# Attention block with two layer norms: two chunks of the rotation move to GpSimd, and the written-out order changes

## The chip, the core and the metric

The kernel runs on one core of a Trainium2 chip. The metric is device time in microseconds (us), from one launch to its end. The engines are TensorE (PE; its weight loads are PEld), VectorE (DVE), ScalarE (ACT), GpSimd (POOL) and SyncE (SP), which here only issues DMAs.

## What is computed

One transformer layer on 2048 tokens of width 128, all in float32: causal attention with 16 heads of width 8 and rotary positions, a residual and a layer norm, then a dense layer with int4-rounded weights plus a low-rank term, a residual and a layer norm.

```python
qkv = einsum('bsd,ed->bse', x, W_qkv)            # x: (1, 2048, 128)
q, k = rope(q), rope(k)                          # pairs of neighbours rotated
scores = q @ k.T / sqrt(8), causal               # 16 heads, 2048 x 2048
out = softmax(scores) @ v                        # the maximum of each row is subtracted
x = layernorm(x + out @ W_o.T)                   # no scale, eps 1e-5
w = clip(round(kernel / s), -8, 7) * s           # s = max|kernel| / 7
x = layernorm(x + x @ w + bias + (x @ a) @ b)
```

## The kernel before

**Tiling.** The tokens are cut into 4 chunks of 512 (`NC`, `CH`), each of 4 tiles of 128, the heads into 4 groups of 4 (`HG`). A task is the queries of one chunk for one group; the last one (group 3, chunk 0) is halved, which makes 17 tasks, 0 to 16. Groups 0 and 2 go through the chunks upwards, 1 and 3 downwards (`TASKS`).

**Two passes over the scores.** Pass A finds each query's maximum: TensorE writes the scores, queries on partitions, into one of two slots of two PSUM banks (`ring`), and VectorE reduces 1024 columns at once (`row_max`, L896). One such piece is a unit; there are 273. Units on the diagonal need the causal mask. In tasks 0 to 3 TensorE adds it by a bfloat16 matmul into the same bank (L1075, L1079); in tasks 4 to 16 (`VECTOR_MASKS`) VectorE adds it while it takes the maximum, one operation a part (`masked_max`, L870). When a task's units are done, its maxima are transposed, split into two parts and written by GpSimd's DMA into extra rows of the query operand (event M: `rows`, `load_maxima`, L749). Then pass S computes the scores again, keys on partitions, with the maximum subtracted by those rows: TensorE writes a set of one or two heads into one of three banks (`sT`, L1110), ScalarE takes the exponential (L814), GpSimd zeroes the masked half of diagonal pieces (L740), and PV multiplies by the values (L1125) into one bank. O normalises (L1134, L940, L942). For group 3 the steps POST 2 to 5 and NORM 0 and 1 follow, with the reciprocal root on GpSimd (`post_rstd`, L712, L715) and the bias there (`post_bias`, L720).

**The start.** TensorE transposes the weights and chunk 0, ScalarE copies them out, and per chunk c and operand w (q, k) come P (two projections, L1035, plain and with neighbours swapped), the two multiplications by cosine and sine (`rotate`, DVE L850), R (their sum, L664), H and T (high part on ScalarE, rest on GpSimd) and E (rows placed by a selecting matmul, L1050). D stores the parts to DRAM, G loads them for the later groups. X and V are a chunk's transpose and values.

**The order.** `schedule()` writes one list of events by a beam search: `Course` keeps times for each engine by constants (LOAD, COLUMN, `maxima_time`, LANDING), and of the candidates those with the least idle time, weighted by `WEIGHTS`, are kept. Every engine walks through that list and executes its part of each event in order, waiting on semaphores. Thus a wait of any instruction holds up all that is behind it on its engine. W, the scale of the int4 weights, is put behind the event PV 1 0, and on GpSimd stands between masks. A POST 3 or 5 also places `post_rstd` on GpSimd's queue at that same place of the list.

## Time and profile before

| | us |
|---|---|
| median of 3 runs (478.73 to 485.3) | 483.12 |
| the profiled execution | 482.48 |
| its span, first to last instruction | 480.7 |
| DVE busy in it | 396.8 |
| ACT busy in it | 311.4 |
| PE busy in it, by modelled ends | 444.2 |

What lies around the span is 1.8 us. The mean granted TensorE clock is 0.955 of full speed. Matmuls overlap, so PE's busy time is no measure of its load; what tells is which wait ends last. The page's DVE time counts overlapping instructions once.

### The profile page before, as it was taken

The numbers are of one execution on the slowest core, as the hardware profiler recorded it, in microseconds if no ns is written. First come the engines' busy times: TensorE is split into PE (matmuls) and PEld (weight loads), VectorE is DVE, ScalarE is ACT, GpSimd is POOL, SyncE is SP. The second block draws the span as 40 slices with busy tenths as digits, with TensorE's granted clock in tenths as the row PEclk, the third lists the DMA queues.
The fourth block names the chain that finished last, engine by engine and source line by source line (L and its number), as shares of the span: only waits on it lengthen the run. The fifth ranks groups of instructions, "written<-read, shape, count | busy, mean of one in ns | idle before, by whom it ended". The sixth has DMA issues, their size and how long they took to land.

```text
span 480.7 us, 8224 instructions
## 1 busy us (share of the span) xinstructions
PE 444.2 (92%) x2914; PEld 200.1 (42%) x2914; DVE 396.8 (83%) x827; ACT 311.4 (65%) x630; POOL 108.1 (22%) x178
## 2 busy tenths in 40 slices
PE   4988799699799999999999999999999999999972
PEld 2445454334343344343434543434344434434542
DVE  1789689789989999999889999998999989933466
ACT  2324467278067868778778786767786788689610
POOL 8543511201100030020303311030002002442343
PEclk9999879899969999999999999999999999999975
DMA  7322211110000001110000011100000000000001
GB/s 240 143 89 89 91 39 54 54 54 24 3 0 2 1 14 55 55 54 14 3 2 3 14 55 55 54 11 1 1 2 3 1 3 2 3 24 1 22 1 44
DMA packets 11576, 16.54 MB, mean 34 GB/s; under 512 B 1820, under 2 KB 6700, under 8 KB 11536
## 3 DMA queue, kind: packets, MB, share of 16 engines
q1 hardware_dynamic: 10448, 15.75, 9.2%
q0 software_dynamic: 1088, 0.28, 0.3%
q8 instruction: 23, 0.38, 0.3%
q14 instruction: 17, 0.14, 0.1%
HBM read 10.37 MB, written 5.24 MB: 32 GB/s over the span
## 4 chain that ended last, share of the span: by engine, by line
PE 72%; DVE 10%; issue 9%; ACT 4%; POOL 2%; DMA 2%; SPq 0%; POOLq 0%; DVEq 0%; ACTq 0%
PE sT L1110 26%; PE oP L1125 23%; PE ring L1068 13%; DVE pmax L896 8%; ACT probs L814 3%; PE sT L1035 2%; PE ring L1134 1%; DMA qS<-mrows 1%; PE oP L1035 1%; PE sT L1050 1%; PE ring L1154 1%; DMA a_sb<-in_L_ffn_a_dram 1%; DVE summed L870 1%; POOL rstd L715 1%; POOL probs L740 1%
## 5 line engine op out<-in xcount | busy, mean ns | idle before, releaser
L814 ACT ACTIVATE probs<-sT 128x512 f32<-128x512 f32 (+2 forms) x576 | 285.9, 581 | 92.8 <-PE sT L1110 91.6
L896 DVE TENSOR_REDUCE pmax<-ring 128x2 f32<-128x1024 f32 (+2 forms) x212 | 248.7, 1220 | 29.4 <-PE ring L1068 26.4
L1110 PE MATMUL sT<-qS,kS 64*128 64x512 f32 (+3 forms) x648 | 193.1, 423 | 6.4 <-ACT vP L772 2.8
L1068 PE MATMUL ring<-kS,qS 64*128 64x512 f32 (+3 forms) x640 | 152.9, 428 | 7.6 <-DVE pmax L896 5.7
L1110 PEld LDWEIGHTS sT<-qS,kS 64*128 64x128 f32 x648 | 97.2, 191 | 128.3 <-ACT probs L814 107.6
L1125 PE MATMUL oP<-probs,vP 128*9 128x512 f32 (+3 forms) x1296 | 146.7, 532 | 2.0 <-POOL probs L740 1.9
L1068 PEld LDWEIGHTS ring<-kS,qS 64*128 64x128 f32 x640 | 71.0, 190 | 51.3 <-DVE pmax L896 27.4
L870 DVE CUSTOM_DVE_ANT_0 summed<-ring,tail_mask 128x128 bf16<-128x128 f32 (+3 forms) x192 | 81.5, 486 | 8.1 <-PE ring L1068 7.5
L740 POOL TENSOR_SCALAR_AFFINE_SELECT probs<-probs 128x512 f32<-128x512 f32 x64 | 40.2, 634 | 199.1 <-ACT probs L814 198.9
L749 POOL DMA_DIRECT2D qS<-mrows x34 | 19.7, 582 | 98.5 <-DVE mrows L916 94.6
L1125 PEld LDWEIGHTS oP<-probs,vP 128*9 128x9 f32 x1296 | 20.4, 88 | 42.3 <-issue 23.2
L823 ACT COPY oT<-oP 128x512 f32<-128x512 f32 (+1 forms) x17 | 9.7, 568 | 19.7 <-PE oP L1125 19.7
L870 DVE DVE_READ_ACCUMULATOR2_ANT pmax<- 128x1 f32 x192 | 15.9, 83 | 0.0
L796 ACT CAST qp<-rot 128x512 fp32r<-128x512 f32 x4 | 2.5, 618 | 17.5 <-POOL rot L664 12.0
L940 DVE RECIPROCAL rsum<-ring 128x16 f32<-128x16 f32 (+1 forms) x17 | 4.1, 241 | 10.8 <-PE ring L1134 10.7
L1134 PE MATMUL ring<-ident,oT 128*128 128x128 f32 x64 | 10.6, 287 | 2.4 <-DVE pmax L896 1.3
L664 POOL TENSOR_TENSOR rot<-rot 128x512 f32<-128x512 f32 x6 | 7.6, 1267 | 20.1 <-DVE rot L850 18.1
L1134 PEld LDWEIGHTS ring<-ident,oT 128*128 128x128 f32 x64 | 7.0, 143 | 8.4 <-DVE pmax L896 5.7
L850 DVE TENSOR_TENSOR rot<-oP,cs 128x512 f32<-128x512 f32 x4 | 2.7, 685 | 9.3 <-PE oP L1035 9.2
L715 POOL TENSOR_TENSOR rstd<-rstd,mhalf 128x4 f32<-128x4 f32 (+1 forms) x10 | 9.2, 916 | 0.8
L850 DVE TENSOR_TENSOR rot<-sT,cs 128x512 f32<-128x512 f32 x12 | 8.0, 684 | 1.5 <-PE sT L1035 1.5
L712 POOL TENSOR_SCALAR rstd<-mv 128x4 f32<-128x4 f32 (+1 forms) x10 | 2.3, 231 | 26.6 <-DVE mv L973 26.6
(126 smaller groups left out, 209.1 us busy)
## 6 DMA issues: line engine op xcount, KB each, us to landing
qS<-q_parts SPq DMA_DIRECT2D x52, 64.0 KB
kS<-k_parts SPq DMA_DIRECT2D x52, 64.0 KB
cs<-rope_tables_dram SPq DMA_DIRECT2D x4, 512.0 KB, 7.0
...
qS<-mrows POOLq DMA_DIRECT2D x30, 8.0 KB, 1.8
```

The lines of the kernel that those rows point to most:

```text
L715: nc.gpsimd.tensor_tensor(rstd[i][:, first:end], rstd[i][:, first:end], mhalf[:, first:end], ALU.pow).then_inc(pool_post[n], 1)
L740: pool.affine_select(out=p, in_=p, compare_op=ALU.is_ge, fill=0.0, base=0, pattern=[[0, HG], [1, TOK]], channel_multiplier=-1).then_inc(ma ...
L749: pool.dma_start(qS[at:at + 2 * SHIFT_STEP + 1:2 * SHIFT_STEP, b, c, :, lo:hi].bitcast(fp32), mrows[0:count, n % 2, a, 0:w].bitcast(fp32)) ...
L814: nc.scalar.activation(probs[:, J % PRING, heads[0]:heads[-1] + 1:2, lo:hi], sT[:, at % SBANKS, 0:len(heads) * (hi - lo)].rearrange("p (h ...
L850: nc.vector.tensor_tensor(rot[:, w, i, :], src, cs_sb[c][:, i, :], ALU.mult).then_inc(bank_free[prep_bank_of((kind, c))[0]], 1)
L870: last = nc.vector.tensor_tensor_reduce(summed[:, slot_of(e), hl, at:at + w], ring[:, slot_of(e), hl, at:at + w], tail_mask[:, CH - w:CH], ...
L896: nc.vector.tensor_reduce(dst, src, AX.X, ALU.max).then_inc(unit_free, 1)
L1035: nc.tensor.matmul(bank, weights, xT[:, c, :], start=True, stop=True).then_inc(bank_done[prep_bank_of((kind, c))[0]], 1)
L1068: last = nc.tensor.matmul(ring[:, slot_of(e), hl, at:at + w], qS[rows, b, c, hp, ii * TOK:(ii + 1) * TOK], kS[rows, b, kk, hp, 0:w], start ...
L1110: last = nc.tensor.matmul(sT[:, at % SBANKS, x * w:(x + 1) * w], kS[rows, b, j // TPC, hp, (j % TPC) * TOK:(j % TPC + 1) * TOK], qS[rows, ...
L1125: last = nc.tensor.matmul(oP[VW * h:VW * h + VC, lo:hi], vP[:, j, HG * g + h, :], probs[:, J % PRING, h, lo:hi], start=j == 0, stop=j == T ...
L1134: last = nc.tensor.transpose(ring[:, slot_of(e), 0, t * TOK:(t + 1) * TOK], oT[:, n % 2, t * TOK:(t + 1) * TOK], ident[:, :])
```

## The change

Seven things are changed:

- **Rotation.** For chunks 2 and 3 (`COPIED`) ScalarE copies the four projections to SBUF and GpSimd multiplies them in place; VectorE does so only for chunks 0 and 1.
- **Masks.** The unit "11" (tile 1 of a chunk, both pairs of heads, 4 parts of 256 columns) gets its mask from TensorE in all tasks. It occurs in 15 tasks, 11 of them from task 4 on. VectorE masks 148 parts instead of 192.
- **First DMAs.** The order is now qkv weights, x of chunk 0, tables of chunk 0, then the output weights and `a`. TensorE waits for the first alone; the others' transposes come behind P 0 1 (`side_weights`). ScalarE prepares q's weights before k's, and VectorE copies chunk 0's transpose.
- **RSTD and BIAS** are events of their own, placed when their inputs are due.
- **Banks.** Behind the last task's M the ring gives one slot, two banks, to pass S, which then has five; the events left in the ring use single banks.
- **L**, the low-rank product, is due at 230 instead of 90 in the planner.
- **Planner.** Costs of maxima, of masks and of the steps above, the horizon of choice and the weights are other numbers, so the whole list comes out anew.

```diff
+def vector_masked(n, unit):
+    return n >= NC and unit[0] in ("01", "02", "2", "3")
...
+POST_STEPS = (("POST", 2), ("POST", 3), ("RSTD", 0), ("NORM", 0), ("POST", 4), ("POST", 5), ("RSTD", 1), ("NORM", 1))
+OFF_PE = ("NORM", "RSTD", "BIAS")
...
+                self.dve = at = max(self.dve, ready) + 1.1 * share
...
+                if k == 0:
+                    self.due += ((self.dve + 0.2, "BIAS", n),)
...
+            if kind == "P" and cost and e[0] >= COPIED:
+                self.act = max(self.act, self.pe) + 1.2
...
-                self.due += ((90.0, "L"),)
+                self.due += ((230.0, "L"),)
...
-    if unit[0] == "keys" or n not in VECTOR_MASKS:
-        return 0.113 + 2 * width(n, unit) / 960
-    return sum(2 * (0.13 + p[3] / 960) for p in products(n, unit)[0])
-Course.A_PE = acc(Course.A, lambda x: pair_cost([p[3] for p in products(*x)[0] for _ in range(2)]) + (0.0 if x[1][0] == "keys" or x[0] in VECTOR_MASKS else 0.3))
+    if not vector_masked(n, unit):
+        return 0.15 + 2 * width(n, unit) / 960
+    return sum(2 * (0.24 + p[3] / 960) for p in products(n, unit)[0])
...
-            soon = max(course.pe, min(x[0] for x in choices)) + 0.5
+            soon = max(course.pe, min(x[0] for x in choices)) + 0.8
...
-WIDTH, WEIGHTS = 16, (1.0, 1.0, 1.0)
+WIDTH, WEIGHTS = 16, (1.0, 1.5, 0.5)
...
+LAST_ROWS = UNIT["M", len(TASKS) - 1]
+SLOT, BEFORE = {}, {}
+for e, u in UNIT.items():
+    if u <= LAST_ROWS:
+        SLOT[e], BEFORE[e] = ((u - 1) % 2, 0), u - 2
+    else:
+        SLOT[e], BEFORE[e] = ((LAST_ROWS - 1) % 2, (u - LAST_ROWS - 1) % 2), max(LAST_ROWS, u - 2)
+GIVEN = LAST_ROWS % 2
...
+BANK, HAD, free, last = [], [], list(range(SBANKS)), {}
+for e in SCHEDULE:
+    if e == ("M", len(TASKS) - 1):
+        free = [SBANKS, SBANKS + 1] + free
+    if e[0] == "S":
+        BANK.append(free[0])
+        HAD.append(last.get(free[0]))
+        last[free[0]] = SET[e[1:]]
+        free = free[1:] + free[:1]
...
+        def ring_bank(e):
+            return ring[:, SLOT[e][0], SLOT[e][1], :]
+        def score_bank(at):
+            return sT[:, BANK[at], :] if BANK[at] < SBANKS else ring[:, GIVEN, BANK[at] - SBANKS, :]
...
+            sp.dma_start(wqkv_sb[:, :, :], w_qkv.rearrange("(k p) d -> p k d", p=128)).then_inc(ld_w, 16)
             sp.dma_start(x_sb[:, 0:TPC, :], x_t[:, 0:TPC, :]).then_inc(ld_x[0], 16)
-            sp.dma_start(wqkv_sb[:, :, :], w_qkv.rearrange("(k p) d -> p k d", p=128)).then_inc(ld_w, 16)
-            sp.dma_start(wo_sb[:, :], w_o).then_inc(ld_w, 16)
-            sp.dma_start(a_sb[:, :], lora_a).then_inc(ld_w, 16)
-            for c in range(NC):
+            sp.dma_start(cs_sb[0], tables[:, :, 0:CH].rearrange("w p s -> p w s")).then_inc(ld_cs[0], 16)
+            sp.dma_start(wo_sb[:, :], w_o).then_inc(ld_side, 16)
+            sp.dma_start(a_sb[:, :], lora_a).then_inc(ld_side, 16)
+            for c in range(1, NC):
+                sp.dma_start(x_sb[:, c * TPC:(c + 1) * TPC, :], x_t[:, c * TPC:(c + 1) * TPC, :]).then_inc(ld_x[c], 16)
...
+            if c >= COPIED:
+                eng.wait_ge(turned[w], 2 * (c - COPIED + 1))
+            else:
+                for kind in ROPE[w]:
+                    prep_freed(eng, (kind, c))
...
+            def rotate_copies(c, w):
+                pool.wait_ge(ld_cs[c], 16)
+                for i, kind in enumerate(ROPE[w]):
+                    prep_freed(pool, (kind, c))
+                    pool.tensor_tensor(rot[:, w, i, :], rot[:, w, i, :], cs_sb[c][:, i, :], ALU.mult).then_inc(turned[w], 1)
             for e in SCHEDULE:
                 if e[0] == "M":
                     load_maxima(e[1])
+                if e[0] == "P" and e[1] >= COPIED:
+                    rotate_copies(*e[1:])
...
-                if e[0] == "POST" and e[2] in (3, 5):
-                    post_rstd(e[1], 0 if e[2] == 3 else 1)
-                if e[0] == "NORM" and e[2] == 0:
+                if e[0] == "RSTD":
+                    post_rstd(*e[1:])
+                if e[0] == "BIAS":
...
+            def side_weights():
+                src = prep_read(act, ("L", 0))
+                nc.scalar.copy(wT[:, 2:4, :], src[:, 0:2 * D].rearrange("p (w d) -> p w d", w=2)).then_inc(side_done, 1)
+                evac(("L", 0), aT[:, :], lambda s: s[0:RANK, 256:384])
...
+            def copy_projections(c, w):
+                act.wait_ge(rope_sum[w], c)
+                for i, kind in enumerate(ROPE[w]):
+                    evac((kind, c), rot[:, w, i, :], lambda s: s)
...
+            nc.vector.tensor_copy(xT[:, 0, :], prep_read(dve, ("X", 0))).then_inc(bank_free[prep_bank_of(("X", 0))[0]], 1)
...
-                if kind != "keys" and n in VECTOR_MASKS:
+                if vector_masked(n, unit):
...
-            pe.wait_ge(ld_w, 48)
+            pe.wait_ge(ld_w, 16)
...
+                if c == 0:
+                    pe.wait_ge(w_done, (4, 7)[w])
...
+                if HAD[at] is not None:
+                    pe.wait_ge(exp_done, HAD[at] + 1)
+                elif BANK[at] >= SBANKS:
+                    pe.wait_ge(*RELEASE[LAST_ROWS - 1])
```

What the list does to each engine is seen in its instructions. On GpSimd, chunk 3 (L664 is the sum of the rotation, L669 the split, L749 the DMA of the maxima, L740 the masks). Before:

```order
L664 TENSOR_TENSOR rot<-rot 128x512 x2
L669 TENSOR_TENSOR qp<-rot,qp 128x512
L669 TENSOR_TENSOR kp<-rot,kp 128x512
L749 DMA qS<-mrows 2x8x128 x2
L740 AFFINE_SELECT probs<-probs 128x4x128 x4
```

Of the change, the same place (L810 are the multiplications, L718 the sums, L723 the splits, L803 the DMA, L794 the masks):

```order
L810 TENSOR_TENSOR rot<-rot,cs 128x512 x2
L718 TENSOR_TENSOR rot<-rot 128x512
L803 DMA qS<-mrows 2x8x128 x2
L810 TENSOR_TENSOR rot<-rot,cs 128x512 x2
L718 TENSOR_TENSOR rot<-rot 128x512
L723 TENSOR_TENSOR qp<-rot,qp 128x512
L723 TENSOR_TENSOR kp<-rot,kp 128x512
L794 AFFINE_SELECT probs<-probs 128x4x128 x4
```

Four multiplications are added (four more for chunk 2), and the DMA of task 1's maxima has moved ahead of chunk 3's k.

On GpSimd, the weight scale (L726 to L733, in the change L780 to L787) and what follows it. Before:

```order
L740 AFFINE_SELECT probs<-probs 128x4x128 x4
L726 ISA
L726 ISA wst<-wst 128x1
L731 ISA
L731 TENSOR_SCALAR wst<-wst 128x1
L733 TENSOR_SCALAR wst<-wst 128x1 x3
L740 AFFINE_SELECT probs<-probs 128x4x128 x4
L749 DMA qS<-mrows 2x8x128 x2
```

Of the change:

```order
L794 AFFINE_SELECT probs<-probs 128x4x128 x4
L780 ISA
L780 ISA wst<-wst 128x1
L785 ISA
L785 TENSOR_SCALAR wst<-wst 128x1
L787 TENSOR_SCALAR wst<-wst 128x1 x3
L803 DMA qS<-mrows 2x8x128 x2
L794 AFFINE_SELECT probs<-probs 128x4x128 x5
```

The DMA of task 2's maxima now follows the weight scale at once, ahead of the four masks that stood between.

On TensorE, where chunk 3's projections (L1035) end and pass S (L1110) begins. Before:

```order
L1035 MATMUL sT<-xT,wT 128x512
L1035 MATMUL oP<-xT,wTs 128x512
L1040 MATMUL sT<-wT,xT 128x128 x4
L1089 MATMUL ring<-ident,nmax 16x128
L1040 MATMUL sT<-wT,xT 128x128 x4
L1110 MATMUL sT<-qS,kS 128x512 x2
L1068 MATMUL ring<-kS,qS 128x512 x4
```

Of the change (L1119 projections, L1125 values, L1153 pass A, L1197 pass S):

```order
L1119 MATMUL sT<-xT,wT 128x512
L1119 MATMUL oP<-xT,wTs 128x512
L1153 MATMUL ring<-kS,qS 128x512 x4
L1125 MATMUL sT<-wT,xT 128x128 x8
L1153 MATMUL ring<-kS,qS 128x512 x2
L1197 MATMUL sT<-qS,kS 128x512 x2
```

Seven units of pass A have moved ahead of pass S's first set. Counted over the whole list, 25 units of pass A stand ahead of pass S's first set, where 18 did. Ahead of task 2's first set are 49 (before 43) units, ahead of task 3's 73 in both, with the same sets of S ahead of each (40 and 84). Behind the last M stand 56 sets of S, before 52.

## Rows read from the trace of the kernel before

**Rows 1.** The page's busy line: busy us, share of the span, instructions of each engine.
```profile
PE 444.2 (92%) x2914; PEld 200.1 (42%) x2914; DVE 396.8 (83%) x827; ACT 311.4 (65%) x630; POOL 108.1 (22%) x178
```

**Rows 2.** The chain that ended last, the page: shares of the span by engine.
```profile
PE 72%; DVE 10%; issue 9%; ACT 4%; POOL 2%; DMA 2%; SPq 0%; POOLq 0%; DVEq 0%; ACTq 0%
```

**Rows 3.** A stage: length, busy us of PE, PEld, DVE, ACT, POOL, clock, DMA, GB/s.
```profile
320.00:420.00 100.00, 98.64 (x676) 41.68 (x668) 91.77 (x208) 75.46 (x151) 14.95 (x24) 1.00 0.01 2
```

**Rows 4.** Timeline in the steady part: start, us, engine, line, operation, idle before.
```profile
307.14 2.36 DVE L896 TENSOR_REDUCE pmax<-ring 128x2 f32<-128x1024 f32 x2 [0.23 <-PE ring L1068]
309.74 2.36 DVE L896 TENSOR_REDUCE pmax<-ring 128x2 f32<-128x1024 f32 x2 [0.24 <-PE ring L1068]
...
307.99 1.05 PE L1125 MATMUL oP<-probs,vP 128*9 128x512 f32 x8
```

**Rows 5.** Chain and timeline of the start.
```profile
2.35 3.29 DMA a_sb<-in_L_ffn_a_dram
...
5.78 0.87 PE L1016 MATMUL sT<-ident,wqkv_sb 128*128 128x128 f32 x3 [5.78 <-DMA a_sb<-in_L_ffn_a_dram]
9.05 2.04 PE L1035 MATMUL oP<-xT,wT 128*128 128x512 f32 x2 [1.12 <-ACT xT L772]
23.40 2.35 DVE L896 TENSOR_REDUCE pmax<-ring 128x8 f32<-128x1024 f32 x2 [0.19 <-PE ring L1079]
```

**Rows 6.** Groups by form: out<-in xcount | busy, mean ns | idle before.
```profile
L850 DVE TENSOR_TENSOR rot<-sT,cs 128x512 f32<-128x512 f32 x12 | 8.0, 684 | 1.5 <-PE sT L1035 1.5
...
L664 POOL TENSOR_TENSOR rot<-rot 128x512 f32<-128x512 f32 x6 | 7.6, 1267 | 20.1 <-DVE rot L850 18.1 <-ACT qp L796 2.1
...
L772 ACT COPY xT<-sT 128x512 f32<-128x512 f32 x3 | 1.7, 579 | 0.0
```

**Rows 7.** Timeline: chunk 3's first projection, and where pass S begins.
```profile
47.15 1.08 PE L1035 MATMUL sT<-xT,wT 128*128 128x512 f32 x2
56.18 0.80 PE L1110 MATMUL sT<-qS,kS 64*128 64x512 f32 x2 [2.78 <-ACT vP L772]
57.52 5.84 DVE L896 TENSOR_REDUCE pmax<-ring 128x2 f32<-128x1024 f32 x5 [4.20 <-PE ring L1068]
```

**Rows 8.** The chain while GpSimd computes the weight scale: start, us, what.
```profile
63.88 7.54 issue
81.95 0.27 POOL wst L731
83.33 0.65 POOL probs L740
87.32 0.78 POOL qS L749
88.11 4.64 DMA qS<-mrows
```

**Rows 9.** Timeline of VectorE, tasks 3 and 4's maxima.
```profile
117.34 10.34 DVE L896 TENSOR_REDUCE pmax<-ring 128x2 f32<-128x1024 f32 x9 [0.22 <-PE ring L1068]
```

**Rows 10.** Timeline of a masked maximum of 256 columns and of TensorE's mask.
```profile
403.29 0.42 DVE L870 CUSTOM_DVE_ANT_0 summed<-ring,tail_mask 128x256 bf16<-128x256 f32 x1
403.64 0.42 DVE L870 CUSTOM_DVE_ANT_0 summed<-ring,tail_mask 128x256 bf16<-128x256 f32 x1
...
46.21 0.39 PE L1079 MATMUL ring<-causal,ident_h 128*128 128x256 bf16 x2
46.59 0.50 PE L1068 MATMUL ring<-kS,qS 64*128 64x512 f32 x2
```

**Rows 11.** The end: rows of the last task; waits, total us, times, longest.
```profile
425.56 1.17 POOL L749 DMA_DIRECT2D qS<-mrows  x2 [2.15 <-DVE mrows L916]
...
ACT probs L814 <- PE sT L1110: 6.8, 12, 1.4
...
458.30 0.23 POOL L712 TENSOR_SCALAR rstd<-mv 128x4 f32<-128x4 f32 x1 [5.26 <-DVE mv L973]
460.31 0.62 PE L1125 MATMUL oP<-probs,vP 128*9 128x256 f32 x8 [1.90 <-POOL probs L740]
```

111 lines of the change are left out of this document (65 added, 46 removed).

## The prediction

> **What bounds the kernel now.** I read the page's busy line first. VectorE is busy 396.8 of 480.7 us, ScalarE 311.4; TensorE's 444.2 is no load, since overlapping matmuls are counted to modelled ends [rows 1]. The chain of waits is mostly TensorE's all the same, 72% against VectorE's 10% [rows 2]: TensorE takes the order of the list, and each piece of either pass goes through it. So neither alone is the bound, and the stretches must be looked at one by one.
>
> In the long middle (320 to 420 us) VectorE is busy 91.8 of 100 us, ScalarE 75.5, at the full granted clock [rows 3]. The timeline shows the beat: two reductions of a unit each, 2.36 us, then 0.23 us in which VectorE waits for TensorE, so 2.60 us from pair to pair, of which one PV takes 1.05 on TensorE [rows 4]. VectorE sets nine tenths of that beat; TensorE's fixed order the rest. Before task 3's rows it is VectorE alone: nine units in a row, 10.34 us, 1.15 each, without a gap [rows 9]. At the end, from the last task's rows at 425.56 to 480.7, there is no pass A; ScalarE, TensorE and GpSimd's small steps take turns [rows 11].
>
> **The start.** TensorE's first transposes wait until 5.78 for the last of four DMAs, whose landing took 3.29 us; the first projection comes at 9.05, 3.27 later, behind the transposes and eleven small copies of ScalarE [rows 5]. Now the weights are issued first, some 1.6 us earlier than that last DMA (2.35 less the 0.8 at which the first one went), and TensorE waits for them alone. The transposes come about 1.6 earlier; k's weights, the side weights and the copy of x no longer stand ahead of the first projection, which I estimate at 0.7 more. I take **-2.3 us** for pass A's first unit (23.40 before). The ends are -1.0, if x of chunk 0, now second, lands late, and -3.4, if the whole preparation halves.
>
> **The rotation.** Eight multiplications leave VectorE, 8.0 us for twelve, so 0.667 each: -5.3 us. On ScalarE come eight copies, 0.58 each, 4.6 us, which I cost at nothing: pass S has not begun there, and nothing else fills that engine. Without that cover they would cost just this. On GpSimd come eight operations like its sum, 1.27 us each, 10.1 us [rows 6]. These lie on a path: ahead of pass S, ScalarE and TensorE wait in the list for chunk 3's splits. Before, chunk 3's first projection is at 47.15, and pass S begins at 56.18, after TensorE waited 2.78 for a copy of V; VectorE meanwhile waited 4.20 [rows 7]. In the new list that projection stands behind 3 more units (+3.5), without the 4 multiplications of chunk 2 (-2.7), and after the earlier start (-2.3): about 45.7. From 1.6 us later GpSimd has four multiplications, two sums and two splits, 8 x 1.27, and a DMA's issue, 1.1: 58.5. So pass S begins **2.4 us later**, but 25 units of pass A stand ahead of it instead of 18.
>
> **Up to task 2's rows.** GpSimd then computes the weight scale. Before it was in this from 63.88 to the next mask at 83.33, most of it "issue", the first piece of 7.54 us [rows 8]. It starts as soon as the masks of task 0 are through, 7.7 us behind pass S's start, so now at 66.2, and lets the next through at 85.6. The DMA of task 2's rows stands right behind it and takes 0.78 + 4.64 as before: task 2's pass S begins at 91.1, before at 87.32 + 5.42 = 92.8 [rows 8]. That is -1.7, with 49 units done instead of 43 and the same 40 sets. The six are worth most just there, since up to task 3 VectorE is the bound: 6 x 1.15 = -6.9 [rows 9]. Together **-8.6 us** up to task 3's first set, where both lists have 73 units and 84 sets behind them. It is also the check on the parts: start and rotation give -7.6, and -1.0 is wait saved. The early start and the rotation are inside this and not counted again. The ends: -2, if GpSimd is 4 us later and half of the lead is lost; -12, if the DMA lands 3 us sooner.
>
> **The masks.** On VectorE parts of 256 columns follow each other after 0.345 us, though each lasts 0.42 (they overlap) [rows 10]. Four make 1.38 us; one reduction instead, 1.18 [rows 4]. Eleven units: -2.2 us, far less than the lengths added up would say. On TensorE a mask's two matmuls push the next work from 46.21 to 46.59, 0.38 us [rows 10]: +4.2. Since the beat holds both engines, I take **+1 us**, ends -2.2 and +4.2.
>
> **The end.** Four more sets stand behind the last rows, +2.0, by ScalarE's 311.4 us for 630 instructions, 0.49 each [rows 1]. Two more banks let TensorE write further ahead, and ScalarE waited 6.8 us for scores there [rows 11]. I take half of it, -3.4. GpSimd sat 5.26 us in the statistics' wait with two masks behind it, so that TensorE came to the last PVs at 460.31 and had itself waited 1.90 [rows 11]; RSTD now stands behind those masks: -1.9. Sum **-3.3 us**; ends +2.0 (the last steps' chain of small operations is the bound anyway) and -8.
>
> L at 230 costs nothing: the same few operations of VectorE are moved, not added, and its users stand at the list's end. TensorE's transposes of the side weights are moved too, behind P 0 1, where VectorE's and ScalarE's work on the first chunk covers them; without that cover they cost about the 0.87 us of the first group of three [rows 5].
>
> **Sum.** -8.6 + 1 - 3.3 = -10.9. The profiled execution took 482.48, 0.64 under the median of 483.12: 482.48 - 10.9 = 471.6, rounded to **471.5 us**. About 2% (9.7 us) is what a measurement of this kernel can tell from no change, so 473.5 is the border: the forecast lies just beyond it.
>
> **Rivals.**
>
> *A: the gain is kept whole.* The new order, with the idle time of VectorE weighted by 1.5, also takes a part of the beat's 0.23 us. That beat occurs some 100 times; a fifth of it is 5 us, and the end gives its other bound, 4 more: about **463 us**. For it speaks VectorE's share in rows 3; against it that a PV of 1.05 us still stands between TensorE's pieces.
>
> *B: the planner leaves VectorE too much room, slower.* It now prices a part of 256 columns at 0.24 + 256/960 = 0.507 us, where the trace has 0.345 [rows 10], and a unit's reduction at 1.217, where it is 1.18. If TensorE fits other work into that room, VectorE idles: 148 x 0.16 = 24 us, less the 192 x 0.05 = 10 already there, and 225 x 0.037 = 8 for the reductions: +22. With the masks at their dear end (+3): 471.5 + 25 = **497 us**. It decides in the steady part and turns the sign when over half of that room (11 us) is really left idle. Against it: VectorE takes up a unit as soon as it is written, and a slot is always one ahead.
>
> *C: GpSimd becomes the bound of the first 90 us.* Its two-input operation takes 1.85 times VectorE's [rows 6]; eight of them and the weight scale are now in one queue with task 1's and 2's rows. If its late hand-over costs the whole lead, -8.6 becomes 0: **480 us**. For it: VectorE already idles 4.2 us there [rows 7]. Against it: the seven units moved ahead fill that wait.
> The Trainium skill (GPSIMD Engine Reference, 4.1 Engine selection) advises against just this move, elementwise work of two inputs on GpSimd, as about 2 times slower than on VectorE. The trace agrees on the ratio (1.85). By that rule the sum would end at C's time; it would be wrong here if VectorE is what waits last, as I hold.
>
> *D: only a part comes through*, half of the lead at task 2 and nothing at the end: 482.5 - 4.3 - 2 = **476 us**. For it: every stretch but the first 130 us is one of several engines, and there a saved wait is often given back at the next.
>
> **Chances.** The forecast with what lies near it (466 to 475) 0.42; A 0.16; D 0.20; C 0.14; B 0.08. Of the forecast's share 0.36 lie under 473.5, with A and some of D 0.56. Within 2%: 0.36. Over 492.8: 0.08, B. The range, 461 to 484, leaves out B and the outer part of A and C.
>
> **What would show it.** The start: pass A's first reduction at 21, TensorE's first transpose near 4.2. The rotation: VectorE busy about 389 us, GpSimd 10 us more. Pass S's first set near 58.5 with 25 units done; the DMA of task 2's rows right behind the scale at 86; task 3's maxima done near 119 (nine of them run to 127.7 in rows 9). The last rows at 417 instead of 425.56, and 53 us from there to the end. The prediction is wrong if the pairs of reductions in the middle stand further apart than 2.60 us, or if the first sets of S come after 62.

## The result and the profile after

The changed kernel takes **480.34 us** (median of 20 runs, 478.77 to 483.31) against 484.59 (478.73 to 487.47) for the kernel before in the same runs. Some executions of the kernel before fall into a slower state, and ratios leave such executions out: this one is 0.994, with a 95% interval of 0.991 to 0.997. The change makes it 0.6% faster, where 471.5 us was forecast. The profiled execution spans 477.2 us, before 480.7; differences between stages are made from these two.

Each trace is of one execution. The changed kernel and the 16 experiments made from it run the same code up to the first reduction, and it comes between 19.75 and 20.90 us; in the two kernels with the start of before it comes at 22.43 and 23.40. So a difference of about 1 us between two traces may be scatter.

The page's busy line, its chain by engine, and the window of the long middle (columns as in [rows 1], [rows 2] and [rows 3]):

```profile
PE 438.2 (92%) x2936; PEld 195.4 (41%) x2936; DVE 391.9 (82%) x743; ACT 316.6 (66%) x637; POOL 117.8 (25%) x186
...
PE 73%; issue 9%; POOL 7%; DVE 5%; ACT 4%; DMA 1%; POOLq 0%; SPq 0%; DVEq 0%; ACTq 0%
...
320.00:420.00 100.00, 97.12 (x650) 40.93 (x638) 90.67 (x189) 75.34 (x149) 12.07 (x21) 0.97 0.01 2
```

VectorE lost 4.9 us of work, GpSimd gained 9.7, and GpSimd's share of the chain rose from 2% to 7%. The middle reads nearly as before; TensorE's clock is 0.97 in it instead of 1.00. The times of four events divide the span. Rows mean GpSimd's first DMA of a task's maxima; the last column is from the last rows to the span's end.

| kernel | first reduction | first set of S | task 3's rows | last rows | middle | end |
|---|---|---|---|---|---|---|
| before | 23.40 | 56.18 | 130.09 | 425.56 | 295.5 | 55.1 |
| after | 19.94 | 64.41 | 128.30 | 423.55 | 295.3 | 53.7 |
| forecast | 21 | 58.5 | 121.5 | 417 | 295.5 | 53 |

So of the forecast 8.6 us up to task 3 only 1.8 came. The middle gave nothing, where +1 was forecast, and the end gave 1.5 instead of 3.3. The forecast spoke of task 3's first set, where both lists have the same work behind them, and the answer is the same there: ScalarE's first exponential of task 3 is at 132.16, before at 133.94. Task 2's is at 100.49, before at 93.55.

**The start** came out at least as well as forecast. Timeline of SP's queue, TensorE and VectorE (start, us, engine, line, operation, idle before):

```profile
0.79 0.45 SPq L652 DMA_DIRECT2D wqkv_sb<-in_L_attn_W_qkv_dram  x1
...
3.50 0.66 PE L1094 MATMUL sT<-ident,wqkv_sb 128*128 128x128 f32 x2 [3.50 <-DMA wqkv_sb<-in_L_attn_W_qkv_dram]
...
6.32 2.04 PE L1119 MATMUL sT<-xT,wT 128*128 128x512 f32 x2 [0.88 <-DVE xT L919]
...
19.94 1.23 DVE L974 TENSOR_REDUCE pmax<-ring 128x8 f32<-128x1024 f32 x1 [0.19 <-PE ring L1164]
```

Transposes go 2.3 us earlier, the first reduction 3.5 [rows 5].

**The lead is lost on GpSimd.** Its timeline, chunk 2 and then chunk 3:

```profile
29.43 2.49 POOL L810 TENSOR_TENSOR rot<-rot,cs 128x512 f32<-128x512 f32 x2 [5.81 <-ACT rot L834]
...
33.21 1.37 POOL L803 DMA_DIRECT2D qS<-mrows  x2
34.59 2.50 POOL L810 TENSOR_TENSOR rot<-rot,cs 128x512 f32<-128x512 f32 x2
37.17 1.26 POOL L718 TENSOR_TENSOR rot<-rot 128x512 f32<-128x512 f32 x1
38.39 1.26 POOL L723 TENSOR_TENSOR qp<-rot,qp 128x512 fp32r<-128x512 f32 x1
...
53.63 2.50 POOL L810 TENSOR_TENSOR rot<-rot,cs 128x512 f32<-128x512 f32 x2 [12.73 <-ACT rot L834]
...
63.59 1.26 POOL L723 TENSOR_TENSOR kp<-rot,kp 128x512 fp32r<-128x512 f32 x1
```

Between 29.43 and the end of q's split at 39.65 GpSimd never rests: two multiplications, a sum, a row DMA, and then k's multiplications and sum stand ahead of q's split, since the list has both projections before both splits. The rows of TensorE, ScalarE and VectorE say who waits:

```profile
39.90 0.74 PE L1135 MATMUL oP<-qp,pick 128*128 128x512 f32 x2 [3.77 <-POOL qp L723]
...
51.68 1.13 PE L1119 MATMUL sT<-xT,wT 128*128 128x512 f32 x2
...
62.52 0.62 ACT L864 CAST kp<-rot 128x512 fp32r<-128x512 f32 x1 [4.32 <-POOL rot L718]
63.05 1.06 ACT L834 COPY vP<-sT 128x512 f32<-128x512 f32 x2
...
64.41 0.80 PE L1197 MATMUL sT<-qS,kS 64*128 64x512 f32 x2 [4.38 <-ACT vP L834]
...
42.90 5.04 DVE L974 TENSOR_REDUCE pmax<-ring 128x8 f32<-128x1024 f32 x4 [5.06 <-PE ring L1164]
...
65.67 1.23 DVE L974 TENSOR_REDUCE pmax<-ring 128x2 f32<-128x1024 f32 x1 [4.37 <-PE ring L1153]
```

TensorE waits 3.77 us and VectorE 5.06. Chunk 3's first projection, forecast at 45.7, is at 51.68, and pass S begins at 64.41 instead of 58.5. The releaser named there, a copy of V on ScalarE at 63.05, itself stands in the list behind the cast at 62.52, which waited 4.32 us for GpSimd's sum. The first wait costs twice, as the windows from 40 to 50 us show (before, then after; the clock is the third number from the end):

```profile
40.00:50.00 10.00, 9.85 (x51) 5.42 (x52) 9.20 (x10) 3.45 (x7) 1.29 (x2) 1.00 0.29 107
```

```profile
40.00:50.00 10.00, 9.96 (x37) 5.31 (x38) 5.25 (x5) 2.68 (x5) 0.90 (x1) 0.52 0.29 107
```

After the 3.77 us TensorE has 0.52 of its clock from 40 to 50, hence mostly the 1.2 GHz level. The clock is low from 60 to 70 too (0.72) and from 90 to 100 (0.75), but there the kernel before has 0.72 and 0.83, so that is hardly new.

**The weight scale** then starts 9.7 us later than in [rows 8] (the chain of waits: start, us, what):

```profile
73.56 8.60 issue
82.15 0.41 POOL wst L780
...
82.63 10.41 issue
93.04 0.27 POOL wst L785
...
96.47 1.02 PE oP L1212
```

It was forecast to end at 85.6; it ends at 94.46, task 2's rows go at 94.41 (forecast 86), and the masks behind them make TensorE wait 3.43 us for its PV at 96.47.

**The end** (waits after 423 us: engine line <- releaser: us in all, times, longest):

```profile
ACT probs L887 <- PE ring L1197: 4.0, 7, 1.3
ACT probs L887 <- PE sT L1197: 2.3, 2, 1.8
...
PE oP L1212 <- POOL probs L794: 0.8, 2, 0.7
```

ScalarE's wait for scores is 6.3 in all. From its last rows to its end the kernel before has 5.9 (the 6.8 of [rows 11] are of 420 to 458 us), so this wait did not shrink. TensorE's for the last masks is 0.8 in all in place of a single 1.90 [rows 11].

### The profile page after: what moved, and what is told of

The parts are those of the page before. It is cut to its first block, busy times and chain, and to the rows that moved or that the text cites. A ratio compares the mean times of both kernels' runs of the same rounds, so it can differ in the third digit from the quotient of the medians.

```text
span 477.2 us, 8198 instructions
## 1 busy us (share of the span) xinstructions
PE 438.2 (92%) x2936; PEld 195.4 (41%) x2936; DVE 391.9 (82%) x743; ACT 316.6 (66%) x637; POOL 117.8 (25%) x186
## 4 chain that ended last, share of the span: by engine, by line
PE 73%; issue 9%; POOL 7%; DVE 5%; ACT 4%; DMA 1%; POOLq 0%; SPq 0%; DVEq 0%; ACTq 0%
PE oP L1212 25%; PE sT L1197 24%; PE ring L1153 15%; DVE pmax L974 4%; ACT probs L887 3%; POOL rot L810 2%; PE sT L1119 1%; PE ring L1221 1%; PE ring L1164 1%; POOL rstd L769 1%; PE sT L1135 1%; POOL rot L718 1%; POOL probs L794 1%; DMA x_sb<-in_L_attn_x_dram 1%; PE ring L1174 1%
## 5 line engine op out<-in xcount | busy, mean ns | idle before, releaser
L887 ACT ACTIVATE probs<-sT 128x512 f32<-128x512 f32 (+1 forms) x553 | 277.5, 581 | 93.2 <-PE sT L1197 90.5
L974 DVE TENSOR_REDUCE pmax<-ring 128x2 f32<-128x1024 f32 (+2 forms) x223 | 262.4, 1221 | 37.5 <-PE ring L1153 25.6
L1197 PE MATMUL sT<-qS,kS 64*128 64x512 f32 (+3 forms) x617 | 174.0, 417 | 7.0 <-ACT vP L834 4.4
L1153 PE MATMUL ring<-kS,qS 64*128 64x512 f32 (+3 forms) x640 | 154.9, 431 | 5.1 <-DVE pmax L974 4.5
L1197 PEld LDWEIGHTS sT<-qS,kS 64*128 64x128 f32 x617 | 88.4, 189 | 106.2 <-ACT probs L887 89.6
L1153 PEld LDWEIGHTS ring<-kS,qS 64*128 64x128 f32 x640 | 71.5, 191 | 59.1 <-DVE pmax L974 31.3
L794 POOL TENSOR_SCALAR_AFFINE_SELECT probs<-probs 128x512 f32<-128x512 f32 x64 | 40.2, 635 | 203.8 <-ACT probs L887 203.3
L948 DVE CUSTOM_DVE_ANT_0 summed<-ring,tail_mask 128x384 bf16<-128x384 f32 (+3 forms) x148 | 66.7, 507 | 5.7 <-PE ring L1153 5.1
L803 POOL DMA_DIRECT2D qS<-mrows x34 | 19.6, 578 | 87.8 <-DVE mrows L994 87.8
L810 POOL TENSOR_TENSOR rot<-rot,cs 128x512 f32<-128x512 f32 x8 | 10.0, 1271 | 18.6 <-ACT rot L834 18.5
L887 ACT ACTIVATE probs<-ring 128x512 f32<-128x512 f32 (+2 forms) x23 | 12.1, 581 | 2.7 <-PE ring L1197 2.7
L948 DVE DVE_READ_ACCUMULATOR2_ANT pmax<- 128x1 f32 x148 | 12.3, 83 | 0.0
L1221 PE MATMUL ring<-ident,oT 128*128 128x128 f32 x64 | 10.5, 284 | 1.3 <-ACT oT L896 0.6
L864 ACT CAST kp<-rot 128x512 fp32r<-128x512 f32 x4 | 2.5, 618 | 12.3 <-POOL rot L718 11.4
L1119 PE MATMUL sT<-xT,wT 128*128 128x512 f32 x14 | 8.6, 698 | 1.6 <-DVE xT L919 0.9
L1164 PE MATMUL ring<-causal,ident_h 128*128 128x256 bf16 x46 | 9.7, 295 | 0.0
```

The costliest lines, as they stand in the source:

```text
L794: pool.affine_select(out=p, in_=p, compare_op=ALU.is_ge, fill=0.0, base=0, pattern=[[0, HG], [1, TOK]], channel_multiplier=-1).then_inc(ma ...
L803: pool.dma_start(qS[at:at + 2 * SHIFT_STEP + 1:2 * SHIFT_STEP, b, c, :, lo:hi].bitcast(fp32), mrows[0:count, n % 2, a, 0:w].bitcast(fp32)) ...
L810: pool.tensor_tensor(rot[:, w, i, :], rot[:, w, i, :], cs_sb[c][:, i, :], ALU.mult).then_inc(turned[w], 1)
L887: nc.scalar.activation(probs[:, J % PRING, heads[0]:heads[-1] + 1:2, lo:hi], score_bank(at)[:, 0:len(heads) * (hi - lo)].rearrange("p (h s ...
L948: last = nc.vector.tensor_tensor_reduce(summed[:, slot_of(e), hl, at:at + w], ring[:, slot_of(e), hl, at:at + w], tail_mask[:, CH - w:CH], ...
L974: nc.vector.tensor_reduce(dst, src, AX.X, ALU.max).then_inc(unit_free, 1)
```

## The experiments

Times are medians; a ratio is to the kernel before, in the same runs, with its 95% interval. Unless it says otherwise, an experiment starts from the changed kernel (480.3 us, 0.994). Three theories stood at first: that GpSimd's queue costs the lead before task 3 (G), that any lead is given back in the middle (M), and that VectorE is the bound everywhere (V). M fell in every run with the changed kernel's list: from task 3's rows to the last rows they all take 294.8 to 296.3 us, however early they begin.

### The start alone

`before_with_start`: the kernel before, with the changed order of the first DMAs, of the weights' preparation and the copy by VectorE.

```diff
+            sp.dma_start(wqkv_sb[:, :, :], w_qkv.rearrange("(k p) d -> p k d", p=128)).then_inc(ld_w, 16)
             sp.dma_start(x_sb[:, 0:TPC, :], x_t[:, 0:TPC, :]).then_inc(ld_x[0], 16)
...
-        PREP = [("W", 0), ("L", 0), ("X", 0)]
+        PREP = [("W", 0), ("X", 0)]
```

> The kernel before, in its own order, with the new start alone: qkv weights first, TensorE waits for them alone, side weights behind P 0 1, x of chunk 0 copied by VectorE. Pass A's first reduction comes near 20 instead of 23.4. If the gain is kept it is 0.993 of before, 481 for 484.5; if the next GpSimd or DMA wait gives it back (theory M or the weight scale's block), 0.998 to 1.0.

Measured: 481.5 us, 0.998 (0.994 to 1.003), so no difference that the times can show. In the trace the first reduction is at 21.05, task 3's rows at 127.63 (-2.5), the last rows at 422.05 (-3.5). This trace is of the fastest of the twelve executions (477.6 us), and its end, with the list of before, is 53.75 us where the kernel before has 55.14. So the markers say that the early start is kept, the times don't prove it, and 1.4 us of an end may be scatter.

### The rotation back on VectorE

`rot_on_dve`: the list stays as it is (`COPIED` is still 2 in the planner), but no chunk is copied and multiplied by GpSimd.

```diff
-COPIED = 2
+COPIED, COPIED_RUN = 2, 4
...
-                if e[0] == "P" and e[1] >= COPIED:
+                if e[0] == "P" and e[1] >= COPIED_RUN:
                     rotate_copies(*e[1:])
```

> The changed kernel with its own order of events, but VectorE multiplies all four chunks by cosine and sine, straight from the banks; ScalarE's eight copies and GpSimd's eight multiplications are gone. Theory G (GpSimd's queue in the first 65 us takes back what the start and the lead give): TensorE's wait of 3.77 us for chunk 2's split and VectorE's of 5.06 behind it go, pass S begins near 58 instead of 64.4, task 3's rows are sent near 123 instead of 128.3, and the time is 475 to 478. Theory M (the middle is set by TensorE's fixed order, which gives any earlier start back): task 3's rows come earlier, the last rows still at 423 to 424, the time 479 to 481. Theory V (VectorE is the bound everywhere): 5.3 us more work on it, 482 to 486.

Measured: **472.4 us**, 0.983 (0.978 to 0.988), better than the 475 to 478 of theory G. Chunk 3's first projection is at 46.38 in place of 51.68, and task 3's rows are at 119.55, 8.75 earlier than in the changed kernel; middle (296.2) and end (53.1) are the same. The stretch of the big waits now (PE, DVE, and the window):

```profile
56.98 0.50 PE L1197 MATMUL sT<-qS,kS 64*128 64x512 f32 x2 [1.27 <-ACT vP L834]
...
39.87 4.62 DVE L974 TENSOR_REDUCE pmax<-ring 128x8 f32<-128x1024 f32 x4 [0.36 <-PE ring L1164]
...
40.00:50.00 10.00, 8.15 (x43) 4.07 (x41) 9.75 (x12) 1.86 (x3) 0.00 (x0) 1.00 0.14 51
```

VectorE's 5.06 us of waiting are 0.36, the clock is whole, and the 5.2 us that VectorE works more (16 multiplications of 0.68 us in place of 8) cost nothing visible, so V fell too. That one move, with ScalarE's copies and GpSimd's multiplications, is the dear part.

`chunk3_on_gpsimd` sets `COPIED_RUN` to 3, so that only chunk 3 goes by GpSimd.

> The changed kernel, but chunk 2 is again multiplied by VectorE straight from TensorE's banks; only chunk 3 goes by ScalarE's copies and GpSimd. The list is the same. Theory H (GpSimd's queue): the loss of the new order has two parts there, chunk 2's split queued behind k's multiplications (TensorE waits 3.77 us at 39.90, VectorE 5.06 at 42.90), and the late split of chunk 3's k. With chunk 2 back, the first wait goes, chunk 3's first projection comes near 47 instead of 51.68, the first set of S near 60 instead of 64.41, the DMA of task 2's rows near 90 instead of 94.41, and the time is 475 to 477 us, half way from 480.3 to the 472.4 of both chunks on VectorE. Rival (chunk 3 alone is the trouble, since pass S waits for it): the first set of S stays at 63 to 64 and the time at 479 to 481. Rival (the copies and multiplications cost by their mere number): a half each, which the markers would show as a first set of S near 60.5 but without the wait at 39.90 being the thing removed.

Measured: 477.6 us, 0.989 (0.984 to 0.995); chunk 3's first projection at 46.66, first set at 59.72, task 2's rows at 90.14, task 3's at 123.18. Of the 8.75 us of GpSimd's rotation 5.1 belong to chunk 2 and 3.6 to chunk 3, which keeps a wait of 4.80 us before pass S.

`split_early`: in the list of the first chunks the split of chunk 2's q stands ahead of k's projection.

```diff
-            (29.0, 1.8, "P", 2, 0), (29.0, 0, "R", 2, 0), (30.0, 1.8, "P", 2, 1), (30.0, 0, "R", 2, 1), (31.0, 0, "D", 1),
-            (32.0, 0, "H", 2, 0), (32.0, 0, "T", 2, 0), (33.0, 0, "H", 2, 1), (33.0, 0, "T", 2, 1), (33.0, 0.9, "V", 0), (34.0, 0.5, "X", 3),
+            (29.0, 1.8, "P", 2, 0), (29.0, 0, "R", 2, 0), (29.0, 0, "H", 2, 0), (29.0, 0, "T", 2, 0), (30.0, 1.8, "P", 2, 1), (30.0, 0, "R", 2, 1), (31.0, 0, "D", 1),
+            (33.0, 0, "H", 2, 1), (33.0, 0, "T", 2, 1), (33.0, 0.9, "V", 0), (34.0, 0.5, "X", 3),
```

> The changed kernel; chunk 2's split of q (H and T) stands right behind its sum in the list, ahead of k's projection, so that GpSimd does it before k's two multiplications. Theory G: TensorE's wait of 3.77 us for it falls under 1, VectorE's 5.06 under 2, the low clock behind it (42 to 50 us) with them, and pass S begins 4 to 7 us earlier than 64.4: 474 to 478. Theory M: pass S as early, but 479 to 481. If k's split, now later, holds TensorE instead: no change in any stage.

Measured: 477.3 us, 0.991 (0.988 to 0.995), first set at 62.45, task 3's rows at 125.03 (-3.3). TensorE's wait falls from 3.77 to 1.77 us, now for k's split, VectorE's from 5.06 to 3.42, and the clock from 40 to 50 is still 0.66. Pass S begins 2.0 us earlier, not the 4 to 7 expected. So queueing q's split behind k's multiplications was about a third of the loss; the rest comes with the other operations in the queue.

### The weight scale

`scale_late` computes it when task 3's first PV is done instead of task 1's.

```diff
-        if event == ("PV", 1, 0):
+        if event == ("PV", 3, 0):
```

> The changed kernel; only the weight scale W is put behind PV 3 0 instead of PV 1 0, where GpSimd otherwise idles for over 20 us. Theory G: task 2's rows and the masks of task 1 no longer stand behind its 20.8 us; the rows' DMA goes out near 86 to 88 instead of 94.4, task 3's near 122 to 124, and the time is 475 to 478. Theory M: the same earlier rows, but 479 to 481 at the end. If the scale only moves its wait to task 3's masks, 480 to 482.

Measured: 474.3 us, 0.987 (0.983 to 0.991), 6.1 less. Pass S begins as late as before (64.97), but task 2's rows go at 86.01 in place of 94.41, and task 3's at 123.24, 5.1 earlier.

`rot_dve_scale_late` does both:

> The changed kernel's order with both: VectorE multiplies all chunks and the weight scale stands behind PV 3 0. Theory G: the two waits lie one behind the other on GpSimd (pass S begins at 57, then the scale), so both gains add in part: task 2's rows go out near 80 instead of 86.8 (rotation alone) or 86.0 (scale alone), task 3's near 116, last rows near 412, time 467 to 470. Rival D (VectorE is the bound from 60 to 120 us once GpSimd no longer is): task 3's rows stay at 118 to 120 and the time at 471 to 473.

Measured: **467.1 us**, 0.968 (0.961 to 0.974); task 3's rows at 116.61, then a middle of 296.0 and an end of 54.5. The two losses nearly add up: 8.0 and 6.1 us alone, 13.3 together. This kernel is the base of several runs below.

### The masks

`masks_all_dve`: the list is the same, but VectorE masks unit "11" again from task 4 on.

```diff
-                if vector_masked(n, unit):
+                if run_masked(n, unit):
+def run_masked(n, unit):
+    return n >= NC and unit[0] != "keys"
```

> The changed kernel in its own order; VectorE masks the unit 11 from task 4 on, as before, in 44 parts of 256 columns. By the spacing of 0.345 us this costs VectorE 2.2 us more and spares TensorE 4.2. From task 3's rows to the last took 295.3 us. If VectorE is what waits last there: 297 to 298, time 481.5 to 483. If TensorE: 292 to 294, time 477 to 479. If the beat is of both and they cancel: 295 and 480 to 481.

Measured: 480.0 us, 0.994 (0.991 to 0.998), as the changed kernel. The times can't show the 1 us forecast for the masks; the dear end of +4.2 is ruled out, and the middle is 294.8 us against 295.3. How the list itself would differ without the change of masks was not run.

### The end

`three_banks`: pass S keeps its three banks; the events left in the ring use single banks as in the changed kernel.

```diff
-    if e == ("M", len(TASKS) - 1):
-        free = [SBANKS, SBANKS + 1] + free
```

> The changed kernel in its own order; pass S keeps its three banks behind the last rows, the two banks given are left unused. From the last rows to the end took 53.7 us. If the five banks give the 3.4 us that I took for them: 56 to 58, time 482.5 to 485. If ScalarE's and GpSimd's own steps set the end: 53.5 to 54.5, time 480 to 481.

Measured: 486.7 us, 1.009 (1.005 to 1.013): the banks are worth 6.3 us by the medians and about 7 by the ratios, more than the 2 to 5 expected. Last rows to end is 59.9 instead of 53.7, and ScalarE waits twice as long for scores:

```profile
ACT probs L885 <- PE sT L1195: 12.2, 16, 2.4
```

`rstd_at_post`: GpSimd computes rstd at the POST steps again, and the bias at NORM.

```diff
-                if e[0] == "RSTD":
-                    post_rstd(*e[1:])
-                if e[0] == "BIAS":
+                if e[0] == "POST" and e[2] in (3, 5):
+                    post_rstd(e[1], 0 if e[2] == 3 else 1)
+                if e[0] == "NORM" and e[2] == 0:
```

> The changed kernel in its own order, except that GpSimd's reciprocal root and bias stand at POST 3, POST 5 and NORM 0 of the list again, ahead of masks that were ready. If that wait is worth the 1.9 us: 54.5 to 56.5 from the last rows to the end, time 481.5 to 483. If the masks behind it had slack: no change, 480 to 481.

Measured: 483.4 us, 1.003 (1.000 to 1.006), 3.0 more (about 4 by the ratios), with an end of 56.3. GpSimd stands again in a wait for statistics, and TensorE waits 2.7 us for the masks behind it, where it was 0.8:

```profile
443.45 0.23 POOL L766 TENSOR_SCALAR rstd<-mv 128x4 f32<-128x4 f32 x1 [8.04 <-DVE mv L1051]
...
PE oP L1212 <- POOL probs L794: 2.7, 2, 2.0
```

### The planner's numbers

The edits so far leave the planner's search alone, and the list is the same but for the moved split and the moved scale. These make a new one. First three on the base of `rot_dve_scale_late`. `plan_all_dve` tells the planner that VectorE rotates all chunks (`COPIED` 4), `true_prices` and `even_weights` change its prices of VectorE's work and its weights (TensorE, VectorE, ScalarE):

```diff
-        return 0.15 + 2 * width(n, unit) / 960
-    return sum(2 * (0.24 + p[3] / 960) for p in products(n, unit)[0])
+        return 0.113 + 2 * width(n, unit) / 960
+    return sum(2 * (0.078 + p[3] / 960) for p in products(n, unit)[0])
...
-WIDTH, WEIGHTS = 16, (1.0, 1.5, 0.5)
+WIDTH, WEIGHTS = 16, (1.0, 1.0, 1.0)
```

> As rot_dve_scale_late, but the planner also knows that VectorE rotates chunks 2 and 3 (it reckons 1.4 us of VectorE for each of their projections), so that the list is made for that engine. Theory H (the queue of GpSimd was the loss, and the list is fine): 465 to 469 us, no change from 467.1 within what is measured. Rival (the list, which puts 25 units ahead of pass S, was made for a rotation off VectorE and is wrong without it): 460 to 464 us, with the first set of S earlier than 57.1.

> As rot_dve_scale_late (rotation of all chunks on VectorE, weight scale after task 3's rows; 467.1 us), but the planner prices reductions as the trace spaces them: 0.113 us + columns/960 for a pair and 0.078 + 256/960 for a part of 256 columns, instead of 0.15 and 0.24. That makes a new list. Theory B (the planner's high prices leave VectorE idle): the stretch from task 3's rows to the last rows falls from 296 us to 285 to 290 and the time to 457 to 462. Theory beat (VectorE's reductions and TensorE's fixed order set the middle; prices don't): last rows 1 to 4 us earlier, but pass S is left behind, so that the end after the last rows is as much longer or more, 467 to 478 us in all.

> As rot_dve_scale_late, but the planner weighs the idle time of its engines evenly (1, 1, 1) as the kernel before did, instead of 1, 1.5 and 0.5; a new list. If the weight on VectorE's idle time is worth something (rival A of the prediction), the stretch from task 3's rows to the last rows becomes longer than 296 us, by up to 5, and the time is 470 to 473. If the beat sets the middle whatever the weights, 296 stays and the time is 466 to 470 us.

Then all prices of before: VectorE's two (0.113 and 0.13), what a mask on TensorE is reckoned to cost (0.3 less in both places that add it) and the horizon (0.5). The four are called the old prices below. They were run with even weights (`old_planner`) and with the new ones (`old_prices_new_weights`); and the new prices with VectorE's weight alone put back (`vector_weight_1`: 1, 1, 0.5).

```diff
-        return 0.15 + 2 * width(n, unit) / 960
-    return sum(2 * (0.24 + p[3] / 960) for p in products(n, unit)[0])
+        return 0.113 + 2 * width(n, unit) / 960
+    return sum(2 * (0.13 + p[3] / 960) for p in products(n, unit)[0])
...
-            soon = max(course.pe, min(x[0] for x in choices)) + 0.8
+            soon = max(course.pe, min(x[0] for x in choices)) + 0.5
```

> As rot_dve_scale_late (467.1 us), but all prices and weights of the planner for pass A are those of the kernel before (0.113 and 0.13, mask 0.3, window 0.5, weights 1, 1, 1). Theory (prices and weights cancel): the stretch from task 3's rows to the last rows is again about 296 us, as in before, and the loss against rot_dve_scale_late is only in the first 125 us: 470 to 474 us. Rival (the new list is better throughout): middle over 300 us and 476 to 482.

> As old_planner, but with the weights 1, 1.5 and 0.5. Its list leaves pass S at 490 sets when the last rows are asked for, where rot_dve_scale_late has 520. If the high prices only serve to keep pass S from falling behind, the last rows come early (middle 285 to 290 us for 408 sets instead of 441) and the end is 12 to 16 us longer: 468 to 474 us. If the order at right prices is better everywhere, 461 to 465 us.

> As rot_dve_scale_late, but weights 1, 1, 0.5: only VectorE's idle time is weighed as before. If VectorE's weight is what counts (even_weights took 482.0 us), the middle is 301 to 305 us and the time 475 to 482. If it is the half weight on ScalarE's idle time, the middle is near 296 us and the time 467 to 471.

Last, the same steps in the two kernels themselves: the changed one with even weights, the changed one with all old prices, and the kernel before with the new weights.

> The changed kernel itself with the weights 1, 1, 1. Its list starts pass S after 21 units instead of 25. If the weights are worth in it what they are in rot_dve_scale_late (15 us), 493 to 496 us, with the middle near 304 us. If the loss by GpSimd hides what the first part of the list is worth (8 us there), only the middle's 8.5 us show: 487 to 490 us.

> The changed kernel, rotation on GpSimd and all, but the planner's prices, mask allowance and window of before (0.113, 0.13, 0.3, 0.5), with the new weights. If the prices cost in it what they cost in rot_dve_scale_late (4.6 us): 475 to 477 us, of it the middle about 273 us for 408 sets and the end 70. If the late start of pass S in this kernel (64.4 us) makes the sets the scarce thing, the gain is lost: 479 to 482 us.

> The kernel before, with the planner's weights 1, 1.5 and 0.5 in place of 1, 1, 1 and nothing else. The same step in the best kernel (old_planner to old_prices_new_weights) gave 8 us, so 475 to 478 us if the weights alone do it, with VectorE busy over 47 of 50 us in the middle. If three score banks can't carry the sets left over at the end, the end after the last rows grows by as much as the middle falls and 481 to 485 us stays.

The sets of pass S that the list has placed when the last rows are asked for, of 576 in all, tell how far pass S lags:

| kernel | prices, weights | us | ratio, interval | task 3's rows | middle | end | sets |
|---|---|---|---|---|---|---|---|
| before | old, even | 484.6 | 1 | 130.1 | 295.5 | 55.1 | 524 |
| rot_dve_scale_late | new, new | 467.1 | 0.968, 0.961-0.974 | 116.6 | 296.0 | 54.5 | 520 |
| plan_all_dve | new, new | 476.4 | 0.988, 0.983-0.993 | 123.4 | 298.6 | 53.1 | 519 |
| even_weights | new, even | 482.0 | 0.998, 0.995-1.002 | 124.8 | 304.6 | 50.6 | 527 |
| vector_weight_1 | new, 1/1/0.5 | 470.0 | 0.973, 0.968-0.978 | 119.2 | 300.1 | 50.3 | 521 |
| true_prices | trace's, new | 471.9 | 0.979, 0.973-0.984 | 116.6 | 270.2 | 86.8 | 454 |
| old_planner | old, even | 470.6 | 0.975, 0.970-0.980 | 120.6 | 292.6 | 53.6 | 517 |
| **old_prices_new_weights** | old, new | **462.5** | 0.957, 0.953-0.961 | 117.5 | 273.0 | 70.1 | 490 |
| changed kernel | new, new | 480.3 | 0.994, 0.991-0.997 | 128.3 | 295.3 | 53.7 | 520 |
| changed_even_weights | new, even | 488.5 | 1.012, 1.006-1.017 | 130.5 | 304.6 | 50.6 | 527 |
| **changed_old_prices** | old, new | 468.3 | 0.967, 0.962-0.972 | 123.6 | 272.7 | 71.0 | 490 |
| before_new_weights | old, new | 485.8 | 1.001, 0.998-1.005 | 126.3 | 288.6 | 69.4 | 512 |

What follows. In the changed kernel the new prices cost **12 us** (480.3 less 468.3) and the new weights give **8** (488.5 less 480.3). Both sizes depend on the rest. On the base of `rot_dve_scale_late` the new prices cost 4.6 us with the new weights and 11.4 with even ones, and the weights give 14.9 us with the new prices and 8.1 with the old. The expectation for `changed_old_prices` had the 4.6 and missed. Its list also starts pass S at 59.67 instead of 64.41 and has task 3's rows 4.7 us earlier, so a part of the 12 us is the same loss as GpSimd's: rotation on VectorE and the late scale together give 13.3 us with the new prices and only 5.8 with the old (468.3 to 462.5).

Prices and weights work against each other in the middle: on that base it is 292.6 us with both old, 273.0 with the new weights, and 296.0 with the new prices as well. A shorter middle isn't all gain, since it leaves more sets to the end.

With the new prices, `vector_weight_1` recovers 12.0 of the 14.9 us that even weights lose, so the half weight on ScalarE gives most of it by the time. Its middle, 300.1, was between the two expectations, and 1.5 on VectorE without the half on ScalarE was not run. Which of the four old prices helps stays open. `true_prices`, VectorE's two lowered further and the rest left, shortens the middle most (270.2), but lags pass S too far (454 sets; the end takes 86.8 us) and loses 4.9 us; 490 sets is the best balance tried. `plan_all_dve`, whose planner knows the engines rightly, is 9.3 us slower: its pass S begins at the same time (56.99 against 57.08), but only 20 units stand ahead of it, not 25. The expectation of no change was wrong; the list that counts on a free VectorE is good even when VectorE is not free.

`before_new_weights` shows that the kernel before gains nothing by the new weights: its middle shrinks by 6.9 us and its end grows by 14.3. ScalarE waits 14.8 us for scores in that end, with three banks and 64 sets left; in `changed_old_prices` it waits 5.6 us, with five banks and 86 sets left. That speaks for weights and banks belonging together. The weights and the five banks alone were not run on the kernel before.

How a list with a low price differs in the middle: VectorE in `changed_old_prices`, with its window,

```profile
307.48 18.27 DVE L974 TENSOR_REDUCE pmax<-ring 128x2 f32<-128x1024 f32 x16
...
320.00:380.00 60.00, 59.52 (x410) 24.34 (x408) 57.30 (x103) 46.51 (x93) 4.80 (x8) 1.00 0.01 2
```

and in the changed kernel, with its TensorE around a pair:

```profile
306.86 2.36 DVE L974 TENSOR_REDUCE pmax<-ring 128x2 f32<-128x1024 f32 x2 [0.23 <-PE ring L1153]
309.45 2.36 DVE L974 TENSOR_REDUCE pmax<-ring 128x2 f32<-128x1024 f32 x2 [0.23 <-PE ring L1153]
...
305.12 1.05 PE L1212 MATMUL oP<-probs,vP 128*9 128x512 f32 x8
306.10 0.49 PE L1197 MATMUL sT<-qS,kS 64*128 64x512 f32 x1
306.10 0.72 PE L1153 MATMUL ring<-kS,qS 64*128 64x512 f32 x2
306.43 0.62 PE L1197 MATMUL sT<-qS,kS 64*128 64x512 f32 x2
306.68 0.60 PE L1153 MATMUL ring<-kS,qS 64*128 64x512 f32 x2
307.28 0.50 PE L1197 MATMUL sT<-qS,kS 64*128 64x512 f32 x1
307.70 1.05 PE L1212 MATMUL oP<-probs,vP 128*9 128x512 f32 x8
```

Two units, four matmuls of S and a PV come every 2.58 us (305.12 to 307.70), and VectorE waits 0.23 of it. In the other list the same stretch has three of S and takes 2.46:

```profile
308.10 1.05 PE L1212 MATMUL oP<-probs,vP 128*9 128x512 f32 x8
309.07 0.50 PE L1153 MATMUL ring<-kS,qS 64*128 64x512 f32 x2
309.41 0.40 PE L1197 MATMUL sT<-qS,kS 64*128 64x512 f32 x2
309.89 0.50 PE L1153 MATMUL ring<-kS,qS 64*128 64x512 f32 x2
310.23 0.39 PE L1197 MATMUL sT<-qS,kS 64*128 64x512 f32 x1
310.56 1.05 PE L1212 MATMUL oP<-probs,vP 128*9 128x512 f32 x8
```

Sixteen reductions then run without a gap. So the beat's gap goes with TensorE's load per pair, which the list sets: a lagging pass S closes it and pays at the end (71.0 us in place of 53.7).

## Why the prediction was wrong

**The step that failed is "-8.6 us up to task 3's first set"**, and in it the -1.7 us at task 2's pass S. Task 3's first exponential came 1.8 us earlier (133.94 to 132.16), not 8.6. Task 2's came 6.9 later (93.55 to 100.49), where 1.7 earlier was forecast; between the two the six units moved ahead gave 8.7, more than the 6.9 forecast.

The error is in the sentence that put chunk 3's first projection at 45.7. It counted TensorE's and VectorE's work ahead of it and nothing of GpSimd's on chunk 2. I priced GpSimd's queue for chunk 3 alone, though chunk 2 runs through the same one and is awaited by TensorE, with q's split behind k's multiplications and a row DMA between. I had the durations right (1.27 us each). The projection came at 51.68, and at 46.38 and 46.66 in the two runs that take chunk 2 off GpSimd. From there to the first set of S it took 12.7 us, which the sum had as 12.8. So nearly all of the 5.9 us by which pass S was late came from chunk 2, with the low clock from 40 to 50 as a part whose size was not isolated.

The markers at task 3's rows divide the 1.8 us in three. The start gives -2.5 there (`before_with_start`), the list another -8.1 (127.63 to 119.55, `rot_on_dve`), and the move to GpSimd takes 8.75 back; each is good to about 1 us, by the scatter of the markers. The first two make -10.5, so lead and early start were not read too high. Undoing the two chunks one after the other divides the 8.75 into 5.1 and 3.6, and shows the second as a cost too, since pass S, the scale and task 2's rows are in line behind it.

**The weight scale** was forecast to begin 7.7 us after pass S and to last 19.4; it began 9.2 after and lasted 20.9, so that 3 of the 8.9 us by which its end was late (94.46 for 85.6) are its own. That it holds the rows back was right. I left it as a fact instead of asking what moving it would give: 6.1 us here (`scale_late`).

**The start**: -2.3 forecast, -3.5 at the first reduction in these two traces. With the scatter of the traces it is -1.5 to -3.7, so the forecast stands.

**The middle** was right in its size and wrong in its reason. I took the beat for a thing of the engines and the planner's new numbers for neutral. Over the whole kernel the weights give 8 us and the prices cost 12, and the masks, +1 with ends -2.2 and +4.2, are nothing that shows. L at 230 was put at nothing and not tried.

**The end**: -3.3 forecast, -1.5 measured, which scatter alone can make. Banks were put at -3.4 and are worth 6.3, rstd at -1.9 and is worth 3.0. What stands against them is the new order of the end, +2.0 forecast, and by difference about +7.5 (-1.5 + 6.3 + 2.7, by the ends of the three spans). What in that order costs this was not isolated; it is the order that keeps the ring to single banks as well. The sum's terms and the markers given with it differ here: -8.6, +1 and -3.3 put the last rows at 418 with 51.8 us behind them, and the prediction names 417 and 53.

**The rivals.** C, GpSimd as the bound of the first 90 us, gave 480 and named the mechanism: the whole lead is lost through late hand-overs. That its number fits to 0.3 us is partly luck, since planner prices and weights that it did not name are in the same time. Against it I had set that seven units moved ahead fill VectorE's wait; VectorE waited 5.06 and 4.37 us all the same, for units that stood behind TensorE's own waits. The rule of the Trainium skill (GPSIMD Engine Reference, 4.1 Engine selection) would have given the better forecast. The trace agrees with it beyond the ratio of durations: 5.2 us saved on VectorE came back as 8 us more in all. Of B's mechanism `true_prices` shows half: lower prices of VectorE's work do close its gaps in the middle, but by themselves they lose at the end. All four prices together are 12 us in place of the 22 worked out. A's weights, put at 5, give 8 and cover a part of it. Neither can be read from the changed kernel's profile alone. D, "half of the lead", named no mechanism.

Of the two limits that I had set, a first set of S after 62 did mark the forecast as wrong. The other one, pairs over 2.60 us apart, did not occur (2.59).
